# A graph network in one core: a third of x1 in three rounded products, low parts of W_ah ahead of x1's, V beside its layer part, the late shifts turned one tile later

## The reference, cut to what matters

```python
# N = 1250 nodes, D = 768, 3 layers of 4 heads with C = 192 features; 41250 edges incl. loops + 1250 loops
x1 = relu(x @ W_ah + b_ah)                       # 1250x768 @ 768x768
for l in 0, 1, 2:                                # the three layers all read x1
    h = (x1 @ W[l]).reshape(N, 4, 192)
    as_n = (h * a_src[l]).sum(-1); ad_n = (h * a_dst[l]).sum(-1)
    e = leaky_relu(as_n[src] + ad_n[dst], 0.2)
    p = exp(e - segment_max(e, dst)[dst])
    xs[l] = relu(segment_sum(p / segment_sum(p, dst)[dst] * h[src], dst) + b[l])
y = relu(concat(xs) @ W_out + b_out)
out = layernorm(x + y)
```

## Time and profile before

| | us |
|---|---|
| median of 3 runs | 944.2 |
| the profiled execution: time; span | 944.62; 943.0 |
| busy: TensorE; weight loads; VectorE; ScalarE; GpSimd | 920.9; 871.6; 740.3; 373.9; 45.8 |
| granted TensorE clock | full in all 40 slices |
| a rounded product of 384 columns, duration of its row | 0.34 |
| a tile of the pairs on TensorE (360 instructions take 58.83) | 3.27 |
| ten feature transposes | 1.07 |
| VectorE in the pairs: from one exponent to the next, with the weight between | 2.80 |
| a late maximum | 1.38 |
| ScalarE: an exponential; the three copies of uT2 | 1.34; 1.27 |

### The profile page before, as it was taken

The page is one execution under the profiler, slowest core; times in us unless marked ns, Lnnn a source line. Parts: engine busy times, 40 slices in busy tenths (PEclk is TensorE's granted clock), DMA queues, the critical chain, the costliest instruction groups (busy, mean ns, idle before and its releaser), DMA issues.

```text
span 943.0 us, 14258 instructions
## 1 busy us (share of the span) xinstructions
PE 920.9 (98%) x5604; PEld 871.6 (92%) x5604; DVE 740.3 (79%) x1068; ACT 373.9 (40%) x564; POOL 45.8 (5%) x94
## 2 busy tenths in 40 slices
PE   6999999999999999999999999999999999999997
PEld 2667689999999999999999999999999999999996
DVE  6999956599999799999999999998887454343232
ACT  1576333222211335565555554555555631010000
POOL 4700000000000000010010010010010100000000
PEclk9999999999999999999999999999999999999999
DMA  5350632543542831343342351339431264233111
GB/s 177 49 201 18 223 114 85 171 141 106 170 143 78 241 129 42 96 138 66 95 120 58 97 132 47 96 86 377 112 103 63 68 161 163 82 111 117 52 33 34
DMA packets 57725, 108.31 MB, mean 115 GB/s; under 512 B 14024, under 2 KB 41265, under 8 KB 56510
## 3 DMA queue, kind: packets, MB, share of 16 engines
q1 hardware_dynamic: 39212, 66.24, 23.1%
q0 software_dynamic: 5360, 18.77, 7.7%
q10 hardware_dynamic: 13090, 22.44, 7.6%
HBM read 80.34 MB, written 27.10 MB: 114 GB/s over the span
## 4 chain that ended last, share of the span: by engine, by line
PE 56%; ACT 0%; DVE 0%; issue 0%; ACTq 0%
PE ps L1420 34%; PE ps L1504 18%; PE ps L1496 2%; PE ps L1455 2%; ACT R_XIN L794 0%; PE ps L1405 0%; DVE R_XIN L1207 0%; DVE stats L1197 0%; DVE R_EXP L1191 0%; DVE R_EXP L1193 0%; ACT rstd L854 0%; DVE mv L1202 0%; DVE rstd L1204 0%; ACTq L793 0%; ACTq L826 0%
## 5 line engine op out<-in xcount | busy, mean ns | idle before, releaser
L1420 PE MATMUL ps<-R_W 125*125 125x193 f32 x2400 | 395.7, 327 | 3.5 <-ACT R_XIN L783 2.2
L1420 PEld LDWEIGHTS ps<-R_W 125*125 125x125 f32 x2400 | 391.6, 188 | 4.7 <-ACT R_XIN L783 2.8
L768 ACT ACTIVATE R_W<-R_EXP,s 125x1250 f32<-125x1250 f32 x120 | 160.5, 1340 | 171.6 <-DVE R_EXP L1058 114.8
L1069 DVE SCALAR_TENSOR_TENSOR R_W<-R_W,R_CNT 125x1250 f32<-125x1250 f32 x120 | 174.5, 1455 | 3.3 <-DVE R_EXP L1058 2.3
L1096 DVE CUSTOM_DVE_ANT_0 R_ROWS<-R_MASK,R_ROWS 125x1250 bf16<-125x1250 bf16 x90 | 124.8, 1456 | 13.6 <-DMA R_ROWS<-as_dram 13.1
L1305 PE MATMUL ps<-Wl_hi,x_hi 128*125 128x384 f32 (+2 forms) x360 | 116.6, 342 | 0.0
L1305 PE MATMUL ps<-Wl_lo,x_hi 128*125 128x384 f32 (+2 forms) x360 | 115.9, 340 | 0.0
L1305 PE MATMUL ps<-Wl_hi,x_lo 128*125 128x384 f32 (+2 forms) x360 | 115.8, 340 | 0.0
L1504 PE MATMUL ps<-Wo_lo,xs_hi 128*125 128x384 f32 (+2 forms) x324 | 109.5, 338 | 0.0
L1504 PE MATMUL ps<-Wo_hi,xs_hi 128*125 128x384 f32 (+2 forms) x324 | 109.5, 338 | 0.0
L1504 PE MATMUL ps<-Wo_hi,xs_lo 128*125 128x384 f32 (+2 forms) x324 | 109.3, 337 | 0.0
(11 more groups left out here) (153 smaller groups left out, 858.5 us busy)
## 6 DMA issues: line engine op xcount, KB each, us to landing
xs_dram<-R_XIN POOLq DMA_DIRECT2D x18, 625.0 KB, 8.2
h_dram<-R_HOUT ACTq DMA_DIRECT2D x30, 336.0 KB
R_W<-h_dram SPq DMA_DIRECT2D x12, 840.0 KB
R_ROWS<-as_dram SPq DMA_DIRECT2D x12, 625.0 KB, 5.4
R_EXP<-u_dram SPq DMA_DIRECT2D x6, 1250.0 KB, 7.5
R_X<-u_dram SPq DMA_DIRECT2D x6, 1250.0 KB, 5.7
R_ROWS<-in_W_all SPq DMA_DIRECT2D x18, 384.0 KB, 3.7
Wo_sb<-in_W_out POOLq DMA_DIRECT2D x1, 6912.0 KB, 27.3
```

What stands on the lines that cost most here:

```text
L768: nc.scalar.activation(prob[r % PSLOTS], expo[:, r % XSLOTS], ACT.Exp, bias=s02[:, r % NT, ds(2 * p + r // NT, 1)]).then_inc(S["exp_done"], 1)
L1069: nc.vector.scalar_tensor_tensor(out=prob[r % PSLOTS], in0=prob[r % PSLOTS], scalar=HUGE, in1=cntT[:, r % NT, 0:N], op0=ALU.min, op1=ALU.m ...
L1420: ins = mm(ps[0:PT, o:o + HW], prob[(q * NT + j) % PSLOTS][:, t * PT:(t + 1) * PT], hB[:, q, j], start=(j == 0 and t % 2 == 0), stop=(j == ...
```

## The change

1. x1's group 1 (500 nodes, a third of the turns and 40% of the columns) is computed in three rounded products per step, with `xg_hi`, `xg_lo` and, per m, `wg_hi` (two buffers) and `wg_lo`. Turns now go group 0, group 2, group 1. ScalarE casts xg_hi in two halves after turns 6 and 7, wg_hi(0) and (1) after turns 8 and 9, the rest each after the turn that frees its buffer. VectorE subtracts xg_lo and wg_lo(0) behind its one-hots, with V's pieces and x1_lo between the further ones.
2. From unit 32 on one step per unit (`x1_upto`) instead of three for four.
3. Each layer's score columns stand in the part of the same number (0, 1, 2), 8 in each; V of layer 2 is made later, the source scores are turned, stored and loaded layer by layer, and `aB` has one buffer, so layer l's vectors are loaded when V of layer l - 1 is done.
4. `shifts(2)` and `shifts(3)` stand before tile 7 of their pair on TensorE, and ScalarE copies at r == 12.

```diff
-X1_ORDER = [(m, 0) for m in range(KT)] + [(m, g) for m in range(KT) for g in (1, 2)]
+X1_ORDER = [(m, g) for g in (0, 2, 1) for m in range(KT)]
+G_AT = {0: 0, 2: KT, 1: 2 * KT}
+SLOW = 36
+SLOW_AT = 31
-SCORED = [2 * ROUND_A, 2 * HEADS]
+SCORED = [2 * HEADS] * LAYERS
+SHIFTS_AT = 7
+SHIFTS_OUT_AT = 12
-V_LAST_AT = 7
+V0_AT = 14
+XG_AT = (6, 7)
+WG_AT = (8, 9)
+V_NEXT_AT = (8, 3)
 def x1_upto(u):
-    return X1_HEAD + 3 * (u + 1) // 4
+    return min(X1_HEAD + 3 * (u + 1) // 4, SLOW) + max(0, u - SLOW_AT)
...
             def load_a(l):
-                if l >= 2:
-                    sp.wait_ge(S["v_made"], 2 * HEADS * KT * (l - 1))
+                if l >= 1:
+                    sp.wait_ge(S["v_made"], 2 * HEADS * KT * l)
...
+            def round_wah(m):
+                act.wait_ge(wah_in[m], 16)
+                nc.scalar.copy(wg_hi[m % 2][:], W_ah_sb[m]).then_inc(S["wg_hi"], 1)
...
                 elif i + 2 - KT < len(GROUPS) - 1:
-                    load_x(i + 3 - KT)
+                    load_x(len(GROUPS) - 1 - (i + 2 - KT))
+                if i in XG_AT:
+                    kk = slice(KT // 2 * XG_AT.index(i), KT // 2 * (XG_AT.index(i) + 1))
+                    act.wait_ge(x_in[1], 16)
+                    nc.scalar.copy(xg_hi[:, kk], xT[1][:, kk]).then_inc(S["xg_hi"], 1)
+                if i in WG_AT:
+                    round_wah(WG_AT.index(i))
+                if G_AT[1] <= i < G_AT[1] + KT - 2:
+                    round_wah(i - G_AT[1] + 2)
...
-            for l in range(2):
-                for k in range(V_HEAD if l == 0 else 0, KT):
-                    reduce_v(l, k)
+            def rest_wah(m):
+                dve.wait_ge(S["wg_hi"], m + 1)
+                dve.wait_ge(S["turn_ps"], G_AT[2] + m + 1)
+                nc.vector.tensor_tensor(wg_lo[m][:], W_ah_sb[m], wg_hi[m % 2][:].bitcast(f32), ALU.subtract
+                                        ).then_inc(S["wg_lo"], 1)
+
+            dve.wait_ge(S["xg_hi"], 2)
+            nc.vector.tensor_tensor(xg_lo[:], xT[1], xg_hi[:].bitcast(f32), ALU.subtract).then_inc(S["xg_lo"], 1)
+            rest_wah(0)
+            reduce_v(0, V_HEAD)
+            rest_wah(1)
+            for k in range(V_HEAD + 1, KT):
+                reduce_v(0, k)
+            rest_wah(2)
             rest_x1(0, 0, KT)
+            for m in range(3, KT):
+                rest_wah(m)
+                if m - 3 < V_TURN:
+                    reduce_v(1, m - 3)
...
-                ins = mm(bank(5 + i % 3)[:, 0:w], W_ah_sb[m][:, k], xT[g][:, k],
-                         start=(k == 0), stop=(k == KT - 1))
+                out = bank(5 + i % 3)[:, 0:w]
+                if g != 1:
+                    ins = mm(out, W_ah_sb[m][:, k], xT[g][:, k], start=(k == 0), stop=(k == KT - 1))
+                else:
+                    for n, (ww, xx) in enumerate(((wg_hi[m % 2], xg_hi), (wg_hi[m % 2], xg_lo), (wg_lo[m], xg_hi))):
+                        ins = mm(out, ww[:, k], xx[:, k], start=(k == 0 and n == 0), stop=(k == KT - 1 and n == 2))
...
-                    if n == 2 and t == 0:
-                        source_turn(1, heads_of[1], GROUPS)
+                    if 2 <= n <= LAYERS and t == 0:
+                        source_turn(n - 1, heads_of[n - 1], GROUPS)
...
                 for r in range(FEAT, 2 * NT if last else 2 * NT + FEAT):
+                    if nth is not None and r == SHIFTS_AT:
+                        pe.wait_ge(S["attT_sb"], 9 * p + 1)
+                        shifts(nth + 1)
...
-            pe.wait_ge(S["attT_sb"], 9 * 2 + 1)
-            shifts(2)
             pair(2, False, nth=1)
```

More of the change, by code:

```diff
@@ L44 @@
 V_TURN = 2
-V_AHEAD = V_TURN + 2
 G0_PARTS = 3
@@ L275, in gnn_program @@
         V = u_place[:, 0:KT * 2 * LH].rearrange("p (k h) -> p k h", k=KT)
-        heads_of = [slice(0, ROUND_A), slice(ROUND_A, LH)]
+        heads_of = [slice(HEADS * l, HEADS * (l + 1)) for l in range(LAYERS)]
         V_part = [V.rearrange("p k (w h) -> p k w h", w=2)[:, :, :, h] for h in heads_of]
@@ L315, in gnn_program @@
             more_in more_chain more_read more_ones more_ps more_stage more_mm more_mask
-            v_made v_hi v_lo x1_lo asad_sb asT_ps asT_sb as_stored
+            xg_hi xg_lo wg_hi wg_lo v_made v_hi v_lo x1_lo asad_sb asT_ps asT_sb as_stored
             max_made scores_ready b_pair_sb uT_ps uT_sb u_stored
@@ L396, in _ @@
                 load_slots(sp, mybir.EngineType.SP, w0, mid, win_in[i])
[L398 to L406, removed]
-                        sp.dma_start(w_raw[0], w_half(0)).then_inc(S["w_in_first"], 16)
+            for k in range(V_HEAD, KT):
+                load_v(0, k)
+            for k in range(VSLOTS - 1):
+                load_v(1, k)
+            load_a(1)
+            for k in range(VSLOTS - 1, V_TURN + 1):
+                load_v(1, k)
+            sp.wait_ge(S["turn_ps"], x1_whole(2))
+            sp.dma_start(w_raw[0], w_half(0)).then_inc(S["w_in_first"], 16)
+            for k in range(V_TURN + 1, V_TURN + VSLOTS):
+                load_v(1, k)
             more, each = passes(sp)
@@ L419, in _ @@
             sp.dma_start(w_raw[1], w_half(1)).then_inc(S["w_in"], 16)
-            for k in range(V_AHEAD, KT):
+            for k in range(V_TURN + VSLOTS, KT):
+                load_v(1, k)
+            for k in range(VSLOTS - 1):
+                load_v(2, k)
+            load_a(2)
+            for k in range(VSLOTS - 1, KT):
                 load_v(2, k)
@@ L799, in pair @@
                     exp_tile(p, r)
-                    if nth is not None and r == NT:
+                    if nth is not None and r == SHIFTS_OUT_AT:
                         act.wait_ge(S["u_stored"], 16 * (2 * nth - 1))
@@ L1025, in _ @@
             for k in range(V_TURN, KT):
-                reduce_v(2, k)
+                reduce_v(1, k)
             rest_w(1)
             rest_v(1)
+            for k in range(KT):
+                reduce_v(2, k)
             def slopes():
-                dve.wait_ge(S["asad_sb"], 2 * NT)
+                dve.wait_ge(S["asad_sb"], LAYERS * NT)
                 nc.vector.tensor_scalar(s08[:], asad[:, :, 0:LH], 1.0 - SLOPE, None, ALU.mult)
@@ L1313, in h_products, with terms @@
                 return ins
-            def hi_terms(t):
-                for i in range(2):
-                    if i == 1:
-                        pe.wait_ge(S["w_lo"], 1)
-                        pe.wait_ge(S["v_lo"], 1)
-                    for k in range(KT):
-                        h_product(0, t, k, i, False)
-            def lo_terms(t):
-                pe.wait_ge(S["x1_lo"], 1 + (t >= 4) + (t >= 8))
+            def terms(t, i, last=False):
+                if i == 0:
+                    pe.wait_ge(S["w_hi"], 1)
+                    pe.wait_ge(S["v_hi"], 1)
+                if i == 1:
+                    pe.wait_ge(S["w_lo"], 1)
+                    pe.wait_ge(S["v_lo"], 1)
+                if i == 2:
+                    pe.wait_ge(S["x1_lo"], 1 + (t >= 4) + (t >= 8))
                 for k in range(KT):
-                    ins = h_product(0, t, k, 2, k == KT - 1)
+                    ins = h_product(0, t, k, i, last and k == KT - 1)
                 return ins
```

107 lines of the change are left out of this document (62 added, 45 removed).

## The result

| | before | after |
|---|---|---|
| median of 6 runs each, us | 944.41 | 938.34 (937.22 to 939.14) |
| ratio, 95% interval | | 0.9936 [0.9926, 0.9947] |
| the profiled execution: time; span | 944.62; 943.0 | 937.93; 936.3 |

A forecast was written before the change was run, and what follows sets the result against it. The prediction took TensorE, busy 98% of the span, to bound the kernel. From 944.6 us it took 4.0 for x1's stage, added 1.0 for the extra transposes and took 2.1 for late shifts: 939.5, range 937.0 to 943.6.

The forecast's parts named there:

- Rounded products: x1's last third: 108 rounded 500-column products at 0.224 us, 24.2 together instead of 30.2, a gain of 6.0.
- The assumed law: Rounded products on TensorE: columns at 0.4167 ns plus a constant surplus of 15.5 ns each.
- The fillers: x1's steps between units 32 to 51: 11.6 us before and 11.6 now, so nothing gained.
- Behind the units: x1 after the last unit: 0.8 us gained before the mask block, 3.4 from there to the layers' first product.
- ScalarE: Casts queued among the units delay count copies: 0.2 us lost, with 0 and 2 as ends.
- Rival (b): ScalarE's queue holds the units: 2 us lost instead of 0.2, giving 941.3; chance 0.10.
- Low parts: VectorE's low parts for x1's rounded turns are ready with slacks of 0.7 to 1.1 us; nothing charged.
- Rival (a): Low parts come late after a 10.8 us load of attention vectors: 4.1 us lost, 943.6; chance 0.12.
- V beside its layer part: Layer scores 8, 8, 8: one more group of transposes costs TensorE 1.0 us; VectorE's moved V costs nothing.
- Late shifts: Shifts turned one tile later in two pairs remove TensorE's 1.05 us waits: 2.1 gained, tile 10's wait covered.
- rival (c): The shifts' wait returns before tile 10, so that part does nothing: 941.6; chance 0.05.
- Rivals (d) and (e): Rounded products: (d) columns alone, 0.208 us, 937.6, chance 0.10; (e) no overlap, 0.34, 952.0, 0.06 with similar losses.

The follow-up runs named there:

- experiment 6: The changed kernel with each of the 108 rounded products of x1 cut into two of 250 columns: 937.89 us, ratio 0.9933.
- experiment 3: The changed kernel with the old filler rate, three steps to four units throughout: 939.32 us, ratio 0.9947 to the kernel before.
- experiment 2: The changed kernel with x1's group 1 in full float32 again, no casts or low parts: 942.66 us, ratio 0.9981 to the kernel before.
- experiment 4: The changed kernel with denser fillers, five steps to four units from unit 32 on: 937.88 us, ratio 0.9933 to the kernel before.
- experiment 8: The changed kernel with ten small linked operations on VectorE ahead of low part 2 of W_ah: 939.55 us, ratio 0.9957 to the kernel before.
- 10: The changed kernel with only VectorE's order behind the mask changed, fillers as after the change: 937.36 us, ratio 0.9933 to the kernel before.
- Experiment 7: The changed kernel with the layers' scores in two turns and V placed as in the kernel before: 942.34 us, ratio 0.998 to the kernel before.
- experiment 5: The changed kernel with ScalarE's copies of the shifts two tiles later (SHIFTS_OUT_AT 14, not 12): 946.35 us, ratio 1.0022 to the kernel before.
- number 9: The changed kernel with denser fillers and a new VectorE order behind the mask: 936.60 us, ratio 0.9919 to the kernel before.

## Why the prediction was right, point by point

**Rounded products.** Forecast 0.224 apiece and 24.2 us; measured 0.226 inside a turn and 24.73 with the edges of the turns, which I had not counted. The assumed law was wrong (experiment 6), the value between its ends hardly moved by it.

**The fillers.** This is the term that was mis-sized: "20 x 0.58 = 11.6 now. Nothing." Where nothing waits, a 250-column filler takes 0.47 to 0.50 and a 500-column one 0.90 to 0.93, so 9 x 0.91 + 6 x 0.49 = 11.1 stood against 20 x 0.49 = 9.8: 1.3 less. The pair of rows that I had read (84.95 to 85.53) lies in a stretch where VectorE sets the pace, and it was not even the highest there (82.67 to 83.31 is 0.64): while VectorE makes its last eleven one-hots, 77.52 to 89.31, TensorE waits for them. Between 66 and 92 us its weight loads stand idle for one-hots in five places, 1.5 us together; after the change it is one place, 0.3. Timeline of TensorE before the change:

```profile
86.55 0.69 PE L1220 MATMUL ps<-R_EXP 128*125 128x120 f16 x8 [0.36 <-DVE R_EXP L934]
```

So the 0.58 held waiting, and the prediction's premise that TensorE bounds these units throughout failed; experiment 3 shows how little a filler costs where it fills such a wait. Measured, the units end 1.28 earlier, although ScalarE's casts took 0.3 and the changed kernel began 0.2 later (41.69 against 41.51): some 1.8 in place of nothing. The 0.5 beyond the 1.3 would fit the fewer waits, which no run tests by itself. That is why the mask block comes at 92.17 and not near 93.5 to 94.

**Behind the units.** Forecast 0.8 and 3.4. Steps behind the last unit 1.77 where they were 2.60: 0.8. From the first turn behind the mask block to the layers 29.68 (92.77 to 122.45), forecast 29.3, before 32.67: 3.0. The stage as a whole gave 5.07, forecast 4.0.

**ScalarE.** Forecast 0.2 lost; about 0.3 by experiment 2, and the one wait among the last units that names it is 0.25 (85.59). Rival (b) did not happen.

**Low parts.** Forecast ready at 106.4, 110.7, 114.4 and 118.4, with slacks of 0.7 to 1.1. They ended at 105.93, 110.00, 113.37 and 117.46, and TensorE, 1.3 us ahead of forecast, began the turns at 106.08, 110.21 and then 4.1 apart. The turn of low part 2 was held by 0.1 us already, that of low part 3 hardly (its start is 0.21 behind the end of the low part, 0.06 more than the hand-over takes), so the forecast slack of 1.0 was gone, most of it because the fillers' term was wrong and TensorE came early. Charging nothing was right by a hair, which was luck; experiments 4 and 8 show that what TensorE gains beyond this comes back as a wait, and 10 that the 0.1 goes with another order. Rival (a) needed a slow load of the vectors, and none was seen.

**V beside its layer part.** The turn cost 1.06, forecast 1.0. I had V end 2.9 after the source scores landed; in fact VectorE waited 1.96 for them. They landed 49.0 us behind the layers' first product, where they landed 44.5 behind it before: the queue that stores them stood behind the loads of V's pieces. Its timeline after the change (SP issues):

```profile
148.37 14.30 SPq L402 DMA_DIRECT2D R_ROWS<-in_W_all  x4
162.71 0.66 SPq L451 DMA_DIRECT2D as_dram<-R_EXP  x1
...
166.17 3.69 SPq L447 DMA_DIRECT2D R_ROWS<-as_dram  x2
```

I had not followed that queue. It cost nothing: the first shifts end at 296.91 and are wanted at 301.30. Experiment 7 shows what the move bought, a wait of 4.45 us and the clock behind it. I had not weighed this; in my sum the move was a cost of 1.0 alone. The forecast needed this part of the change to come out, and did not know why.

**Late shifts.** Forecast 2 x 1.05; measured 2 x 1.23. The wait in brackets counts from the modelled end of the row before, and in the stream the next product would have started some 0.15 before that end. Timeline before the change, the last features' transposes; the shifts' follow at 487.88:

```profile
485.60 1.23 PE L1455 MATMUL ps<-ident,R_XIN 125*128 125x125 f32 x10
```

The two starts are 2.28 apart where a group in the stream takes 1.07, so the wait cost 1.21. The shifts' transposes themselves take 1.07 from start to start either way. The cover in front of tile 10 held; experiment 5 shows its edge, and there my price for its loss was too low, since I counted the wait (rival (c) put both at the 2.1 of the gain) and not the clock.

**Sum.** -5.07 + 1.06 - 2.46 = -6.5 from the marks, -6.7 in the spans; forecast -4.0 + 1.0 - 2.1 = -5.1. The largest miss is the fillers' term. Rivals (d) and (e) are settled by the 0.226.

## What to carry to other kernels

When the bound engine gets shorter work, ask first whether its suppliers keep up: here the gain in products was good for 5 us, but what came on top stopped at one low part that stood behind a long row of VectorE's work, and a queue with two low parts a piece of V earlier freed 1.3 more, with denser fillers. Read a filler's price from several rows, and from those beside which nothing waits, and ask which engine sets the pace where it goes: beside a waiting TensorE a filler is nearly free. And do not price a wait of TensorE at its length alone: those of 2.37, 2.65 and 4.45 us cost up to 1.6 more, the one of 1.20 did not.

## What the runs showed of the hardware that I had not expected

- Behind waits of 2.65 and 4.45 us TensorE's granted clock stood at 0.50 (1.2 GHz) in stretches of 2.9 and 3.9 us, behind one of 2.37 at 0.52 for 3.5; behind the one of 1.20 in experiment 4 the products kept their 0.22 us. It cost 1.5 to 1.6 us each time. Another execution of experiment 8's kernel kept a mean clock of 0.999, so not each such wait brings it.
- Rounded products with stationary blocks 125 or 128 columns wide take 0.1164 (250 columns), 0.1755 (384) and 0.2263 us (500) from start to start: 6.5 ns and 0.44 ns per column fit all three.
- Executions of one kernel begin in two forms, some 0.6 us apart, told by the transposes at 12 us that last 0.75 or 0.46: in the one TensorE is at 1.2 GHz there (half-products of 500 columns 0.83 us apart up to 19.52 after the change), in the other at 2.4 (0.42 apart from 14.15 on in number 9).
